# Layer 1 of a four-layer model: the routed experts on gathered rows, between heads 13 and 14

## The reference

```python
        TOP_K = 2
        CAPACITY_FACTOR = 1.0
        ...
        capacity = max(1, int(CAPACITY_FACTOR * T / E_r))
        flat_x = x.reshape(T, D)
        shared_sum = jax.vmap(_ffn, in_axes=(None, 0, 0))(flat_x, shared_w1, shared_w2).sum(0)
        ...
        _, topk_idx = jax.lax.top_k(aff, TOP_K)
        mask = (topk_idx[:, :, None] == jnp.arange(E_r)[None, None, :]).any(axis=1)
        score = jnp.where(mask, aff, -1.0).T
        _, sel_idx = jax.lax.top_k(score, capacity)
        ...
        inp = flat_x[sel_idx]
        out = jax.vmap(_ffn)(inp, routed_w1, routed_w2)
        routed_sum = jnp.zeros_like(flat_x).at[sel_idx].add(out * w[:, :, None])
        return (shared_sum + routed_sum).reshape(B, S, D)
```

## Time and profile before

| | |
|---|---|
| median of the runs | 828.32 us (827.7, 828.32, 833.49) |
| span of the profiled execution | 825.5 us |
| PE busy | 751.2 us, 91% |
| DVE, ACT, POOL busy | 554.4, 371.9, 339.0 us |
| heads 0 to 15 | about 233 to 574 us of the span |
| experts, up to the normalised x of layer 2 | 574 to 656 us |
| layers 2 and 3 | 656 to 825.5 us |

### The profile page before, as it was taken

The page is one execution under the profiler, slowest core; times in us unless marked ns, Lnnn a source line. Parts: engine busy times, 40 slices in busy tenths (PEclk is TensorE's granted clock), DMA queues, the critical chain, the costliest instruction groups (busy, mean ns, idle before and its releaser), DMA issues.

```text
span 825.5 us, 12512 instructions
## 1 busy us (share of the span) xinstructions
PE 751.2 (91%) x4180; PEld 590.4 (72%) x4180; DVE 554.4 (67%) x1101; ACT 371.9 (45%) x783; POOL 339.0 (41%) x250
## 2 busy tenths in 40 slices
PE   6999999999979999999999999998999799766467
PEld 2456676667838898989898999997889446455356
DVE  4454554632269979797979675755566844499995
ACT  2554111101146565656565656555455441475541
POOL 0000364420046757575757584843111110337661
PEclk9999999999999999999999999999999999977798
DMA  8300000000040100010100010101110000100001
GB/s 315 154 0 1 1 1 1 1 1 0 1 147 2 27 25 27 24 28 23 28 23 27 24 51 6 33 7 37 41 38 0 0 1 0 33 0 1 0 1 51
DMA packets 11167, 24.33 MB, mean 29 GB/s; under 512 B 1217, under 2 KB 5442, under 8 KB 10626
## 3 DMA queue, kind: packets, MB, share of 16 engines
q1 hardware_dynamic: 10832, 23.02, 8.3%
q10 hardware_dynamic: 306, 0.92, 0.5%
HBM read 22.89 MB, written 1.05 MB: 29 GB/s over the span
## 4 chain that ended last, share of the span: by engine, by line
PE 68%; DVE 21%; issue 7%; ACT 2%; DMA 1%; POOL 1%; DVEq 1%; SPq 0%; ACTq 0%; POOLq 0%
PE bank L467 11%; PE bank L486 8%; PE bank L488 8%; PE bank L487 8%; PE bank L476 7%; PE bank L649 4%; PE bank L556 3%; PE bank L542 3%; PE bank L679 2%; PE bank L504 2%; PE bank L678 2%; DVE x L1422 2%; PE bank L663 2%; PE bank L525 2%; DVE arena L1396 2%
## 5 line engine op out<-in xcount | busy, mean ns | idle before, releaser
L486 PE MATMUL bank<-zone 128*128 128x256 f32 (+1 forms) x520 | 180.2, 346 | 9.2 <-DVE arena L1397 3.9
L488 PE MATMUL bank<-zone 128*128 128x256 f32 (+1 forms) x520 | 169.5, 326 | 0.0
L487 PE MATMUL bank<-zone 128*128 128x256 f32 (+1 forms) x520 | 169.3, 326 | 0.0
L486 PEld LDWEIGHTS bank<-zone 128*128 128x128 f32 x520 | 99.2, 191 | 26.7 <-DVE arena L1397 9.4
L1733 POOL TENSOR_TENSOR arena<-arena 128x512 f32<-128x512 f32 x64 | 82.2, 1284 | 84.4 <-ACT arena L1030 75.5
L488 PEld LDWEIGHTS bank<-zone 128*128 128x128 f32 x520 | 99.1, 191 | 8.7
L487 PEld LDWEIGHTS bank<-zone 128*128 128x128 f32 x520 | 99.4, 191 | 6.6
L1738 POOL TENSOR_TENSOR arena<-arena 128x512 f32<-128x512 f32 x64 | 82.4, 1288 | 33.1 <-DVE arena L1397 23.0
L1727 POOL TENSOR_TENSOR zone<-arena,zone 128x512 fp32r<-128x512 f32 (+1 forms) x56 | 58.6, 1059 | 58.9 <-ACT zone L1092 46.2
L467 PE MATMUL bank<-xT,arena 128*128 128x512 f32 x160 | 77.1, 611 | 0.0
L1049 ACT ACTIVATE arena<-arena 128x256 f32<-128x256 f32 (+1 forms) x128 | 62.1, 487 | 32.9 <-DVE arena L1406 32.8
(11 more groups left out here) (268 smaller groups left out, 1530.4 us busy)
## 6 DMA issues: line engine op xcount, KB each, us to landing
arena<-in_qk SPq DMA_DIRECT2D x16, 256.0 KB, 2.7
arena<-in_tern SPq DMA_DIRECT2D x1, 3072.0 KB, 20.3
arena<-in_wv SPq DMA_DIRECT2D x8, 256.0 KB, 2.6
arena<-in_wo SPq DMA_DIRECT2D x16, 128.0 KB, 2.0
arena<-in_w SPq DMA_DIRECT2D x8, 256.0 KB, 2.7
lB<-in_lB SPq DMA_DIRECT2D x1, 1288.5 KB, 22.9
arena<-in_lA SPq DMA_DIRECT2D x1, 1282.5 KB, 13.6
x<-in_x SPq DMA_DIRECT2D x1, 1024.0 KB, 11.0
```

Source lines behind the costliest of these rows:

```text
L486: pe.matmul(dst, lhi, rhi, start=(n == 0), stop=False)
L487: pe.matmul(dst, lhi, rlo, start=False, stop=False)
L488: last = pe.matmul(dst, llo, rhi, start=False, stop=(n == len(terms) - 1 and not open_end))
```

## The change

The routed experts no longer run over all tokens. Two tables in DRAM are added, `xg_rows` (1024 rows of 256) and `y_rows` (1023 rows of 256, the last one zero). SP clears xg_rows early, in layer 0. In head 9 DVE goes on from wT1: a running count of the kept tokens of each expert gives each its slot, expert x 146 + position (`weigh_tokens`: three more operations of 7 x 1024 and a chained one). After head 10 PE turns both tables (16 transposes, `turn_routes`) and waits for `wcol_ready`, the first two instructions of `find_rows` on DVE; the rest of find_rows (some eleven small chained operations) makes for every token two row numbers and two weights.

In heads 11 and 12 POOL scatters the normalised rows xn1 into xg_rows by 16 indirect DMAs (8 tiles, two choices; numbers out of bounds are skipped), SP loads the table back as xg. After head 13 PE turns xg (16 transposes), runs the shared expert on all 1024 tokens, and the seven routed experts on their 146 rows each: `routed_in`, 12 matmuls of 146 columns, and `routed_out`, 6 matmuls of 256 columns with 73 rows of output, per expert. The shared output is added to x as before. The routed outputs are copied to yg (73 partitions by 7 experts by 512) by ACT (`keep_y`, even experts) and DVE (odd ones), and SP stores them to y_rows in seven DMAs, four once experts 2 and 3 are copied, three once 5 and 6 are. Then heads 14 and 15 run. POOL, after its part of head 14 (`beside_head(SPLIT)`), waits for all seven stores and issues 16 indirect DMAs that fetch two rows per token (`fetch_rows`); DVE, in head 15 before its reciprocal and `rest_of_oT`, waits for all 16 and adds them to x with their weights (`add_experts`, 16 instructions of 128 x 256). The measuring and normalising for layer 2 stand now between head 15's four add_head steps. The weights w1, w2 and the buffers have moved; the shared expert comes first in the weights. The loop over pairs of experts is written out.

```diff
+SLOTS = ER * CAP
+HCAP = CAP // 2
...
+SPLIT = H1 - 2
...
+        xg_rows = nc.dram_tensor("xg_rows", (T, D), F32, kind="Internal").ap()
+        y_rows = nc.dram_tensor("y_rows", (SLOTS + 1, D), F32, kind="Internal").ap()
...
+            sp.wait_ge(kvbd_ready, 1)
+            sp.dma_start(xg_rows.rearrange("(t p) d -> p t d", p=P), kvbd[:, 0:1, :].to_broadcast([P, NT, D])).then_inc(rows_cleared, 16)
+            sp.dma_start(y_rows[SLOTS:SLOTS + 1, :], kvbd[0:1, 0, :]).then_inc(rows_cleared, 16)
...
+            next_wqk(SPLIT)
+            sp.wait_ge(scattered, 2 * NT * 16)
+            sp.dma_start(xg, xg_rows.rearrange("(t p) d -> p t d", p=P)).then_inc(xg_loaded, 16)
+            for n in range(E1):
...
+            for n in range(2, E1):
+                sp.wait_ge(w2e_split[n % 2], n // 2)
+                sp.dma_start(w2e[n % 2], dram["w2"][n]).then_inc(w2e_loaded[n % 2], 16)
+            y_of = y_rows[0:SLOTS].rearrange("(e i p) d -> p e i d", e=ER, i=2)
+            for e0, e1 in ((0, 4), (4, ER)):
+                sp.wait_ge(*g_r2[e1 - 1].ready)
+                sp.wait_ge(*g_r2[e1 - 2].ready)
+                for e in range(e0, e1):
+                    sp.dma_start(y_of[:, e], yg[0:HCAP, e, :].rearrange("p (i d) -> p i d", i=2)).then_inc(y_stored, 16)
...
+            def routed_in(e):
+                a, (i, r) = (e + 1) % 2, divmod(e, PACK)
+                pe.wait_ge(w1e_split[a], (e + 1) // 2 + 1)
+                for n, g in enumerate(g_r1[i]):
+                    if r == 0:
+                        reuse(g)
+                    last = split_product(g.ps[:, r * CAP:(r + 1) * CAP], [(cut(parts(w1e2[a]), ALL, tok(k * KD + n)), cut(parts(xgT), ALL, k, rows_of(e)))
+                                                                          for k in range(KD)])
+                    if r == PACK - 1 or e == ER - 1:
+                        last.then_inc(g.full_sem, 1)
+                    elif n == 1:
+                        last.then_inc(w1_used, 1)
...
+            def routed_out(e):
+                a, g = (e + 1) % 2, g_r2[e]
+                pe.wait_ge(w2e_split[a], (e + 1) // 2 + 1)
+                reuse(g)
+                if e % PACK == 0:
+                    pe.wait_ge(ehid_ready, NB + e // PACK + 1)
+                for i in range(2):
+                    at = slice(e * CAP + i * HCAP, e * CAP + (i + 1) * HCAP)
+                    last = split_product(g.ps[0:HCAP, i * D:(i + 1) * D], [(cut(parts(rhid2), ALL, at), parts(w2e2[a]))])
+                last.then_inc(g.full_sem, 1)
+
...
-                for a in range(2):
-                    pe.wait_ge(w2e_split[a], i + 1)
...
+            pe.wait_ge(xg_loaded, 16)
...
+            pe.wait_ge(*g_tx[NB - 1][KD - 1].ready)
+            for e in range(ER):
+                routed_in(e)
+            shared_out()
+            for e in range(ER):
+                routed_out(e)
+            for left in HEAD1["left"]:
+                pe.wait_ge(*left)
+            head(H1 // 2 - 1, 0, True, True, HEAD1)
+            head(H1 // 2 - 1, 1, False, False, HEAD1)
...
+            def keep_y(e):
+                act.wait_ge(*g_r2[e].full)
+                act.activation(yg[0:HCAP, e, :], g_r2[e].ps[0:HCAP, :], ACT.Copy).then_inc(g_r2[e].ready_sem, 1)
...
+                dve.scalar_tensor_tensor(out=sT[:, 0:T], in0=affT, scalar=const[0:ER, C_OFF:C_OFF + 1], in1=sT0,
...
+            def find_rows():
+
+                dve.wait_ge(bank_full[0], TURNED)
+                step(dve.tensor_copy(kwt, ps[0][:, 0:NT * ER].rearrange("p (t e) -> p t e", t=NT)), dve_done)
+                k = step(dve.tensor_copy(ktab, ps[0][:, NT * ER:2 * NT * ER].rearrange("p (t e) -> p t e", t=NT)), dve_done)
...
+            def add_experts():
+
+                dve.wait_ge(gathered, 2 * NT * 16)
+                for s in range(2):
+                    for t in range(NT):
+                        if s:
+                            dve.wait_ge(combined, t + 1)
+                        dve.scalar_tensor_tensor(out=x[:, t, :], in0=got[s][:, t, :], scalar=wtok[:, s, t:t + 1], in1=x[:, t, :],
+                                                 op0=ALU.mult, op1=ALU.add).then_inc(combined, 1)
...
+                    x_is(4 * h + base["added"])
+                    add_experts()
                 dve.wait_ge(exp_done, h * 4 + 4)
...
-                    add_head(h, p)
+                    if last:
+                        dve.wait_ge(combined, NT + 2 * p + 2)
+                    add_head(h, p, base)
...
+                add_pair(g_s2[p], p)
+            for e in range(1, ER, 2):
+                dve.wait_ge(*g_r2[e].full)
+                dve.tensor_copy(yg[0:HCAP, e, :], g_r2[e].ps[0:HCAP, :]).then_inc(g_r2[e].ready_sem, 1)
+            head(SPLIT, base=HEAD1)
+            head(H1 - 1, more=False, base=HEAD1, last=True)
...
+            def send_rows(ns):
+                for n in ns:
+                    pool.indirect_dma_start(xg_rows, bass.IndirectOffsetOnAxis(idx[:, n:n + 1], 0), xn1[:, n % NT, :], None,
+                                            bounds_check=SLOTS - 1, oob_is_err=False).then_inc(scattered, 16)
+
+            def fetch_rows(ns):
+                for n in ns:
+                    pool.indirect_dma_start(got[n // NT][:, n % NT, :], None, y_rows, bass.IndirectOffsetOnAxis(idx[:, n:n + 1], 0),
+                                            bounds_check=SLOTS, oob_is_err=False).then_inc(gathered, 16)
...
                         rest_of_wv(i + 1)
-            beside_head(H1 - 2)
+            for h in range(SPLIT - 4, SPLIT):
+                if h == SPLIT - 3:
+                    pool.wait_ge(rows_cleared, 32)
+                    pool.wait_ge(idx_ready, 1)
+                first_row = (h - SPLIT + 3) * 8
+                sends = first_row in (0, 8)
+                beside_head(h, between=(lambda: send_rows(range(first_row, first_row + 4))) if sends else (lambda: None))
+                rest_of_wqk(h + 2)
+                if h % 2 == 0:
+                    rest_of_wv(h // 2 + 1)
+                if sends:
+                    send_rows(range(first_row + 4, first_row + 8))
+
+            def rest_of_w1(n):
...
+            for n in range(2, E1):
+                rest_of_w2(n)
+            beside_head(SPLIT, HEAD1)
+            pool.wait_ge(y_stored, ER * 16)
+            fetch_rows(range(2 * NT))
             rest_of_wo(H1 - 1)
-            with pool.Fori(0, E1 // 2) as i:
```

More of the change, by code:

```diff
@@ L764, in _ @@
[L764 to L779 removed]
+            head(SPLIT // 2 - 2, 0)
@@ new lines, in _ @@
+            turn_routes()
+            pe.wait_ge(wcol_ready, 1)
+            head(SPLIT // 2 - 2, 1)
+            head(SPLIT // 2 - 1, 0)
+            head(SPLIT // 2 - 1, 1)
+            pe.wait_ge(xg_loaded, 16)
+            for b in range(NB):
+                for k in range(KD):
+                    g = g_tx[b][k]
+                    reuse(g)
+                    for tt in range(TPB):
+                        last = pe.transpose(g.ps[:, tok(tt)], xg[:, b * TPB + tt, tok(k)], ident)
+                    last.then_inc(g.full_sem, 1)
@@ new lines, in _ @@
+            round_w1(0)
+            for b in range(NB):
+                for k in range(KD):
+                    g = g_tx[b][k]
+                    act.wait_ge(*g.full)
+                    act.activation(xgT[0][:, k, b * BW:(b + 1) * BW].bitcast(F32R), g.ps, ACT.Copy).then_inc(xg_hi, 1)
+            round_w1(1)
+            round_w2(0)
+            for b in range(NB):
+                expert_silu(b, g_s1[b][1], BW)
+            round_w1(2)
+            for b in range(NB):
+                expert_hi(b, shid2[0][:, b * BW:(b + 1) * BW], BW)
```

418 lines of the change are left out of this document (254 added, 164 removed).

## The result

The changed kernel takes 853.57 us (median of 4 runs, 852.88 to 856.18) against 828.04 us for the kernel before beside it: ratio 1.0299, 95% interval 1.0271 to 1.0326, slower by 3%. The profiled run has a span of 854.2 us and is the longest of the four (the others 850.9 to 852.0); the profiled run before has 825.5.

What follows compares the result with a forecast made beforehand. PE was taken to bound heads and experts. The expert stage, stores, fetches, adds and bare tail reached 673 us, plus 7 beside the heads made 680 against 655.7 (+24.3); span 849.8 plus 2.8 gave 852 us, range 820 to 870.

Steps and rivals of the forecast that it cites:

- the likeliest case: All seven 73-partition stores go through one DMA engine: 852 us; the forecast range 840 to 865 had chance 0.69.
- point of comparison: Last normalisation at the end of layer 1: forecast at 680 us against 655.7 before, +24.3.
- the 2.8 us put on top for the median: Whole kernel: added to the forecast span of 849.8 us because the earlier median was 828.32 against a span of 825.5.
- Beside the heads, 7 us: Work added beside the heads before the expert stage: weigh_tokens 1 us, turn_routes and find_rows 4, scatters 2.
- Head 13's idle 8.84 us takes most of it; I put 2 us on PE: Scatters in heads 11 and 12: 5.6 us beyond POOL's free 13.6, mostly absorbed in head 13, 2 us left.
- The stage, 38.2 us: Expert stage from head 13's end at 543.8 to head 14's start at 582: 38 us where 82 stood.
- an upper bound of 0.25: Routed experts: a 146-column product costs at most 0.25 us, at the plain fp32 rate; 0.12 was taken.
- The stores: Seven stores of the experts' rows on one engine: issued about 577, 51 us at 50 ns a row, landed 630.
- The fetches, 21.5 us: After the stores, POOL issues 16 fetches at 1.2 us, 19.2, plus 2.3 for the last to land: 651.5.
- The adds and the bare tail: End of layer 1: add_experts 6.4 us to 658, then reciprocal, project_out, adds, measures and normalisations uncovered, to 673.
- spread stores, 820 us: Rival: 73-partition stores go to many engines and land by 586, before POOL is free at 597; 820 us, chance 0.17.

Runs made afterwards that it cites:

- e2_no_scatters: The changed kernel with its 16 scatters beside heads 11 and 12 left out, all else the same: 845.72 us, ratio 1.0191 to the kernel before.
- e1_spread: The changed kernel with the experts' row stores cut into 64 partitions per expert, partitions 64 to 72 in separate DMAs: 829.06 us, ratio 0.9992 to the kernel before.

## Why the prediction was right, and where its terms were off

The forecast was the likeliest case, one engine for the stores, at 852 us; measured 853.6. Its point of comparison, the last normalisation, was put at 680 us and came at 685.5. Errors of up to 6.5 us, partly against each other, make up the 5.5 us. So the mechanism was right, and that the number came within 2 us is in part luck: the errors add up to 19 us if their signs are left out, and the 2.8 us put on top for the median did not come, since the profiled run was the longest of the four.

- **Beside the heads, 7 us: it was 12.7.** The step that failed is "Head 13's idle 8.84 us takes most of it; I put 2 us on PE". The reckoning set the scatters against POOL's free time summed over two heads, wherever it lay. But four of them a head stand ahead of rest_of_wo, on which loads, roundings and products hang in a row, and idle time behind an instruction can't hide what stands ahead of it. By e2_no_scatters they cost 10.1 us where 2 stood. turn_routes and find_rows were put at 4 us and cost 2.2. The remaining 0.4 lies ahead of head 10, where 1 us stood for weigh_tokens.
- **The stage, 38.2 us: 41.8 (+3.6, from head 13's end to head 14's start).** Turns, shared_in and the 0.11 us of a 146-column product at full clock were right, against an upper bound of 0.25. But PE's clock was at half for 17 us, where a product of 146 or of 256 columns takes 0.213 us alike: routed_in took 17.7 instead of 16, shared_out 5.0 instead of 2.9. The sum reckoned with full clock throughout. What brought the clock down stays open.
- **The stores.** Issued when the last w2 load was away, as said, at 593.3 (577 + 7 was forecast, and the two errors above are the difference). One engine, as said: landed at 639.8, 46.5 us for 1022 rows, 45.5 ns each where the earlier trace rows gave 50. That is 6.5 us less than the 53 that stood there with issue and landing. The stores came some 6.4 us after one another, POOL waited 26.26 us, PE's clock was at half behind it.
- **The fetches, 21.5 us: 23.4 (+1.9).** POOL is held 1.00 us by one and 0.30 goes by before the next: 1.30, where 1.2 was taken out of 0.43 to 2.5. The last took 3.6 us to land instead of 2.3. The Trainium skill's 1 us ("DMA: Bandwidth & Descriptors", section "Latency and other measured facts") was cited for the first byte, which no run here shows. Taken as the price of one DMA it would have given an estimated 16 us for the sixteen, 5 us too low.
- **The adds and the bare tail.** 6.3 us and 16.0, where 6.4 and 15.1 stood. The path through PE was as drawn, with one wait that the prediction had not named: wo's load for head 15 stood behind the stores on SP, ACT stood at its rounding, and PE at the last weigh_values until 640.26 us (18.40). It cost nothing, since the fetches ended later still.

The sum: 5.7 + 3.6 - 6.5 + 1.9 - 0.1 + 0.9 = 5.5 us, and 1.1 back behind the last normalisation: 849.8 + 5.5 - 1.1 = 854.2, the span of the profiled run. The rival "spread stores, 820 us" had its condition right and its price wrong by 9 us: e1_spread is at 829, since the 12.7 us and the longer stage stand there too. So with spread stores the change makes no difference that can be measured (0.9965 to 1.0019), and no gain.

## What to carry to other kernels

Look at the partition count of every DMA that a change adds: 72 or 64 with a small rest is 24 us faster here than 73. Idle time of an engine covers new work only if the new work stands behind the instructions that others wait for; so put it where the idle time lies in the order of time, and don't go by a sum over heads. When rows come in late at the end of a stage, order the adds so that only the last tile hangs on the last arrival.
